# Row products of the scores on 64 rows, four in a burst, and seven PSUM banks in one rotation

## What is computed

```python
def _L0_cond_ref(x, mask, conditioning, Wq, Wk, Wv, Wo, rms_scale, Wc, bc):
    q, k, v = (proj(Wq), proj(Wk), proj(Wv))            # (B, 16, 512, 16)
    scores = jnp.einsum('bhsd,bhtd->bhst', q, k) * scale
    scores = jnp.where(mask[None, None, :, :], -jnp.inf, scores)
    attn = jax.nn.softmax(scores, axis=-1)
    out = jnp.einsum('bhst,bhtd->bhsd', attn, v)
    out = out.transpose(0, 2, 1, 3).reshape(B, S, E)
    out = out @ Wo.T
    ...
```

## Time and profile before

| what | us |
|---|---|
| median of 3 runs | 1162.19 (1161.24 to 1168.41) |
| the profiled execution, its span | 1162.1 |
| attention: first row product to last column product | about 18 to 613 |
| experts and the end | 613 to 1162 |

### The profile page before, as it was taken

How to read it: one execution, slowest core, us unless ns; L and a number is a source line. 1 busy time by engine, 2 the same in 40 slices (tenths; PEclk the granted TensorE clock), 3 DMA queues, 4 the chain that set the end, 5 groups by cost and what they waited for, 6 DMA issues and landing times.

```text
span 1162.1 us, 23399 instructions
## 1 busy us (share of the span) xinstructions
PE 1122.4 (97%) x7520; PEld 763.4 (66%) x7520; DVE 770.8 (66%) x2265; ACT 803.1 (69%) x1752; POOL 512.6 (44%) x837
## 2 busy tenths in 40 slices
PE   8899999999999999998989999999999999999988
PEld 4333434434334343342418999998999999999968
DVE  4877777787887878878745434355555555667747
ACT  2578888787787877877786756655666666666645
POOL 8424135583755837657462365354222223222220
PEclk8999999999999999999999999999999999999999
DMA  8665638367384572843837488856566766723536
GB/s 220 193 195 189 219 100 250 124 215 231 119 257 138 198 235 94 242 157 133 286 101 269 115 309 306 267 120 133 155 193 190 213 193 179 226 48 70 164 91 217
DMA packets 101616, 213.64 MB, mean 184 GB/s; under 512 B 10917, under 2 KB 71341, under 8 KB 93046
## 3 DMA queue, kind: packets, MB, share of 16 engines
q1 hardware_dynamic: 86038, 192.42, 51.1%
q0 software_dynamic: 14304, 18.69, 9.0%
q10 hardware_dynamic: 1152, 1.05, 0.4%
HBM read 239.28 MB, written 74.29 MB: 270 GB/s over the span
## 4 chain that ended last, share of the span: by engine, by line
PE 46%; ACT 3%; issue 1%; DVE 1%; POOL 1%; DMA 1%; another core or an unknown queue 0%; ACTq 0%; POOLq 0%
PE bank L1084 38%; PE bank L1247 1%; PE bank L1189 1%; PE bank L1099 1%; ACT pt L1355 1%; PE bank L1170 1%; DMA x<-yout,rows 1%; PE bank L1113 1%; PE bank L1174 1%; PE bank L1207 1%; PE bank L1282 0%; PE bank L1155 0%; PE bank L1227 0%; ACT full L1433 0%
## 5 line engine op out<-in xcount | busy, mean ns | idle before, releaser
L1628 DVE CUSTOM_DVE_ANT_0 junk<-bank,mneg 128x512 bf16<-128x512 f32 x512 | 333.0, 683 | 119.0 <-PE bank L1155 116.3
L1355 ACT ACTIVATE pt<-bank 128x512 f32<-128x512 f32 x512 | 301.0, 594 | 67.8 <-PE bank L1170 29.7
L1975 POOL DMA_INDIRECT x<-yout,rows x78 | 122.8, 1574 | 292.9 <-ACT yout L1438 249.6
L1084 PE MATMUL bank<-hid,w 128*128 128x256 f32 x1872 | 242.7, 286 | 4.2 <-DVE hid L1776 3.8
L1084 PEld LDWEIGHTS bank<-hid,w 128*128 128x128 f32 x1872 | 229.3, 190 | 6.0 <-issue 4.8
L1776 DVE TENSOR_TENSOR hid<-full,hid 128x256 fp32r<-128x256 f32 x312 | 133.3, 431 | 135.3 <-ACT full L1433 126.8
L1428 ACT ACTIVATE hid<-bank,biases 128x256 fp32r<-128x256 f32 x312 | 149.4, 479 | 91.6 <-PE bank L1084 88.0
L1433 ACT ACTIVATE full<-bank,biases 128x256 f32<-128x256 f32 x312 | 148.7, 477 | 0.0
L1174 PE MATMUL bank<-mneg,identb 128*128 128x512 bf16 x386 | 146.9, 381 | 0.0
L1084 PE MATMUL bank<-rowsT,w 128*128 128x256 f32 x936 | 122.9, 284 | 0.9 <-issue 0.9
L1084 PE MATMUL bank<-w,hid 128*128 128x256 f32 x936 | 121.9, 283 | 1.5 <-DVE hid L1776 1.5
(11 more groups left out here) (184 smaller groups left out, 1445.2 us busy)
## 6 DMA issues: line engine op xcount, KB each, us to landing
w<-split_weights SPq DMA_DIRECT2D x80, 1024.0 KB
w<-split_weights SPq DMA_DIRECT2D x40, 2048.0 KB
split_weights<-w_parts SPq DMA_DIRECT2D x64, 512.0 KB, 3.8
w_parts<-in_W SPq DMA_DIRECT2D x64, 256.0 KB, 4.3
split_parts<-parts SPq DMA_DIRECT2D x28, 384.0 KB, 2.6
rows<-routed SPq DMA_DIRECT2D x39, 258.0 KB, 3.4
stacks<-split_parts SPq DMA_DIRECT2D x36, 256.0 KB, 5.2
qst<-split_parts SPq DMA_DIRECT2D x24, 256.0 KB, 5.3
```

The lines of the kernel that those rows point to most:

```text
L1084: product = T.matmul(ps, w[p], x[q], start=(k == 0 and n == 0), stop=(k == len(weights) - 1 and n == 2))
L1355: A.activation(pt[n % len(pt)][:, :], bank[3 + n % 2][:, :], ACT.Exp, scale=float(D) ** -0.5).then_inc(exped.sem, 1)
L1628: V.tensor_tensor_reduce(junk[n % 2][:, :], bank[n % 3][:, :], mneg[:, 0, st, :], 1.0, FLOOR, ALU.add, ALU.max, rowmax[gi % 2][:, hh, st:s ...
L1975: G.indirect_dma_start(x2_dram, bass.IndirectOffsetOnAxis(ap=rows[j % NS][:, tt, E + 1:E + 2].bitcast(U32), axis=0), yout[j % NY][:, tt], ...
```

## The change

- The row product takes only the first four of the six pairs (`ROW_PAIRS`): 64 rows instead of 96. The heads of a group are laid out in two halves. Heads 0 and 1 have their four pairs on partitions 0 to 63, heads 2 and 3 on 64 to 127. The other two pairs, the shift rows and zeros fill the other half, so that a column product takes 98 rows for heads 0 and 1 as before, and all 128 for heads 2 and 3.
- The four row products of a step `k` are issued one after another, ahead of its column products, in head order 0, 2, 1, 3: alternately on the lower and the upper 64 partitions. For the first two groups they stay single, the lower half's first.
- All products of the attention except "weigh" take banks 0 to 4, 6 and 7 in one rotation (`RING`), in the order in which they are issued. Each waits for its bank's last user seven places back. A seed is chosen so that the last user was a column product, and ScalarE writes it up to three column products ahead.
- With the layout, the DMAs into `qst` and `kst` are split in two halves (24 instead of 12 per sequence, 2 instead of 1 for each group's maxima), and POOL writes six more constants. For the first two groups the projections of the second sequence come one `k` earlier, and splitting and turning of maxima move by a few places.

```diff
+ROW_PAIRS = 4
+KR = ROW_PAIRS * D
+ROW_HEADS = (0, 2, 1, 3)
+RING = (0, 1, 2, 3, 4, 6, 7)
+SEED_AHEAD = 3
-SEEDED_HEADS = (3,), (0,), (3,), (0,)
-FIRST_PROJECTS = range(3, 7)
+FIRST_PROJECTS = range(2, 6)
...
+def slot_of(h):
+    g, hh = divmod(h, GH)
+    return hh // 2 * (H // 2) + g * (GH // 2) + hh % 2
+
+def pair_rows(half, r):
+    if r < ROW_PAIRS:
+        first, step = half * KR + r, ROW_PAIRS
+    else:
+        first, step = (KR, KR // 2)[half] + r - ROW_PAIRS, len(PAIRS) - ROW_PAIRS
+    return slice(first, first + (D - 1) * step + 1, step)
+
+def shift_rows_of(half):
+    return slice(0, SHIFTS) if half else slice(KQ, KQ + SHIFTS)
...
+    first_rows = [(i, hh, st) for n in range(2) for i in range(2) for st in range(ST) for hh in (2 * n, 2 * n + 1)]
...
+            if 2 <= i < GROUPS:
+                out.append(("rows", i, k))
             for n in range(GH):
-                if i < GROUPS:
-                    out.append(("row", i, n, k))
-                if k == 0 and n == 0 and 0 <= i - 1 < GROUPS:
+                if i < 2:
+                    found = first_rows[(i * ST + k) * GH + n]
+                    out.extend((("one_row", *found), ("row", *found)))
+                elif i < GROUPS:
+                    out.append(("row", i, ROW_HEADS[n], k))
+                if n == 0 and ((i, k) == (1, 2) or k == 0 and 2 <= i <= GROUPS):
                     out.append(("split_maxima", i - 1))
...
-            if k == 1 and 0 <= i - 1 < GROUPS:
-                out.append(("maxima_rows", i - 1))
+                if (i, k, n) == (1, 2, 2) or (k, n) == (1, 3) and 2 <= i <= GROUPS:
+                    out.append(("maxima_rows", i - 1))
...
+    def ring_before(step):
+        n = ring_place[step] - len(RING)
+        return ring_users[n] if n >= 0 else None
+
+    seed_after = {}
+    for gi in range(1, GROUPS):
+        for kt in range(ST):
+            choices = []
+            for hh in range(GH):
+                before_it = ring_before(("col", gi, kt, hh))
+                if before_it[0] == "col":
+                    choices.append((col_place[gi, kt, hh] - col_place[before_it[1:]], -hh))
+            if choices:
+                ahead, hh = max(choices)
+                place = col_place[gi, kt, -hh]
+                seed_after[cols_at[place - min(ahead, SEED_AHEAD)]] = gi, kt, -hh
...
+    def ring_bank(step):
+        user = ring_before(step)
+        return bank[RING[ring_place[step] % len(RING)]], user and evicted(user)
...
                     for r in range(n, len(PAIRS), STACK_STEPS):
-                        start((qst, kst)[qk][b % 2][r:KQ:len(PAIRS), :, :].rearrange("d (a h) s -> d a (h s)", a=2),
-                              split_dram[b, qk, PAIRS[r][qk]].rearrange("(a d h) s -> d a (h s)", a=2, d=D)).then_inc(dma_stack[qk], 16)
+                        for half in range(2):
+                            start((qst, kst)[qk][b % 2][pair_rows(half, r), half * (H // 2):(half + 1) * (H // 2), :],
+                                  split_dram[b, qk, PAIRS[r][qk]][half * P:(half + 1) * P, :].rearrange("(d h) s -> d h s", d=D)
+                                  ).then_inc(dma_stack[qk], 16)
...
+        def row_product(gi, hh, st):
+            b, half, at_slot = gi // NG, hh // 2, slot_of(gi % NG * GH + hh)
+            ps = take(ring_bank(("row", gi, hh, st)))
+            stacks_loaded(pe, b, half)
+            rows = slice(half * KR, (half + 1) * KR)
+            T.matmul(ps[:, :], qst[b % 2][rows, at_slot, st * P:(st + 1) * P],
+                     kst[b % 2][rows, at_slot, :], start=True, stop=True).then_inc(row_scored.sem, 1)
...
-                n = row_place[gi, hh, st]
-                if n >= 3:
-                    pe.wait_ge(*max_found.at(rows_at[n - 3]))
-                stacks_loaded(pe, b, h // (H // 2))
-                T.matmul(bank[n % 3][:, :], qst[b % 2][0:KQ, h, st * P:(st + 1) * P], kst[b % 2][0:KQ, h, :],
-                         start=True, stop=True).then_inc(row_scored.sem, 1)
+            elif name == "one_row":
+                row_product(*at)
+            elif name == "rows":
+                gi, st = at
+                for hh in ROW_HEADS:
+                    row_product(gi, hh, st)
             elif name == "col":
                 gi, kt, hh = at
-                ps = bank[3 + n % 2]
+                stack = slice(0, P) if hh // 2 else slice(0, KQ + SHIFTS)
+                ps, freed = ring_bank(step)
                 seed = (gi, kt, hh) in seeded.value
                 if seed:
                     pe.wait_ge(*seeded.at((gi, kt, hh)))
                 else:
-                    pe.wait_ge(*(exped.at(cols_at[n - 2]) if n >= 2 else v_ready.at((0, ST - 1))))
+                    pe.wait_ge(*freed)
```

More of the change, by code:

```diff
@@ L1 @@
+import struct
 import numpy as np
@@ L816, in stacks_loaded @@
             for qk in range(2):
-                queue.wait_ge(dma_stack[qk], 16 * len(PAIRS) * b)
+                queue.wait_ge(dma_stack[qk], 2 * 16 * len(PAIRS) * b)
     def first_rows(qk, half, part, r):
         assert PAIRS[r][qk] == part
-        return ((qst, kst)[qk][0][r:KQ:len(PAIRS), half * (H // 2):(half + 1) * (H // 2), :], parts[qk][:, half, part, :])
+        return ((qst, kst)[qk][0][pair_rows(half, r), half * (H // 2):(half + 1) * (H // 2), :], parts[qk][:, half, part, :])
     def last_col(b):
@@ L966, in sync_program @@
                     sp.wait_ge(*last_col(b - 2))
-                start(qst[b % 2][KQ:KQ + SHIFTS, gi % NG * GH:(gi % NG + 1) * GH, :], mrow[gi % 2][:, :]).then_inc(dma_mrow[gi % 2], 16)
+                sp.wait_ge(constants_made, CONSTANTS)
+                for half in range(2):
+                    first, n = slot_of(gi % NG * GH + half * GH // 2), SHIFTS * GH // 2
+                    start(qst[b % 2][shift_rows_of(half), first:first + GH // 2, :],
+                          mrow[gi % 2][half * n:(half + 1) * n, :]).then_inc(dma_mrow[gi % 2], 16)
             elif name == "pads":
@@ L1817, in constant, with shift_constants @@
             made[0] += 1
+        def shift_constants(i):
+            halves = [slice(half * (H // 2), (half + 1) * (H // 2)) for half in range(2)]
+            for stacks in (kst, qst):
+                constant(G.memset, stacks[i][0:KR // 2, halves[1], :].bitcast(F32), 0.0)
+            for half in range(2):
+                constant(G.memset, kst[i][shift_rows_of(half), halves[half], :].bitcast(F32), TWO_MINUS_ONES)
         G.memset(ident[:, :], 0.0).then_inc(ident_made, 1)
```

84 lines of the change are left out of this document (46 added, 38 removed).

## The result

The changed kernel takes 1192.51 us (median of 4 runs, 1192.12 to 1195.23), the kernel before 1162.82 on the same chip: ratio 1.0251, 95% interval 1.0225 to 1.0276. It is **slower by 2.5%**. The forecast was 1138. The profiled execution has a span of 1190.4 us, 28.3 more than before.

A forecast was written before the change was run, and what follows sets the result against it. The prediction took TensorE to bound the attention, streaming 96% of its middle part. From 1162.1 us it took 18 (bursts), 0 (rotation), 4 (end) and 2 (start), giving 1138 us, range 1125 to 1150.

The forecast's parts named there:

- The bound: Middle of the attention: TensorE streams 96% of the time, idles about 20 of 480 us, and the readers wait.
- The burst, 0.73 us (0.65 to 0.85): Four paired 64-row products on TensorE, with mode entry and exit, take 0.73 us instead of 0.876.
- Rivals 3: Each mode change on TensorE drains the product's tail: 0.86 us per burst, total 1154 us; chance 0.10.
- 4 (no pairs, 1.09): 64-row products do not run side by side: 1.09 us per burst, total 1181 us; chance 0.09.
- The gain, 18 us: Attention: 0.15 us saved in each of 120 bursts shortens the whole by 18 us (bounds 3 and 27).
- One rotation, 0 us (+10 to -15): Seven banks shared in the attention: new waits of 9 us and 11 us of removed thin waits cancel.
- The wait that I priced: Third column product behind a projection waits 0.33 us for its bank; 28 projections make 9 us.
- Rival 2: The rotation's waits in the attention give back the burst's gain, 24 us; total 1155 to 1164 us; chance 0.14.
- my own sign: TensorE idle growing to 1.5 us per group, with `rests`, `max_rows` or `o_ready` before a column product, shows rival 2.
- The start, -2: Start of the attention, where DVE sets the pace: more maxima queued ahead save 2 us (0 to 3).
- the end, -4: Last two groups of the attention: TensorE runs ahead on seven banks, ACT's gaps close, saving 4 us (2 to 5).
- The signs that I had named: Row products start in pairs, 17.5 us per group in the middle, TensorE idle near 0.8 us per group.

The follow-up runs named there:

- e5: The rotation-only kernel (e1) with the four row products in one burst from the third group on, still on 96 rows: 1200.1 us, 1.0279.
- e6: The changed kernel with each burst of four row products cut into two bursts of two: 1184.67 us, 1.0166.
- e7: The changed kernel with a step's side product (projection and the like) moved between the first and second pair of column products: 1179.73 us, 1.0097.
- e9: The changed kernel with two bursts of two and the side product behind the first column product: 1181.34 us, 1.0139.
- e1: The kernel before with only the one rotation of seven banks, rows and columns alternating on 96 rows: 1171.33 us, 1.0054.
- e8: The changed kernel with VectorE's rest of a projection ahead of the step's first row maximum instead of behind it: 1202.74 us, 1.0317.
- e11: e7 with two steps of the gate's chain put later in VectorE's order for five of eight sequences: 1182.16 us, 1.0149.
- e10: The kernel before with the side product moved between column products, as in e7, as a control: ratio 1.0085.
- e4: The changed kernel with the heads of a burst in the order 0, 1, 2, 3: ratio 1.0285.

## Why the prediction was wrong

**The bound.** Right for the kernel before: TensorE sets its pace. What I did not read from the earlier trace rows is how close behind the others came. VectorE and ScalarE were at 78 and 80% and were fed rows and columns in turn. I took their 99.8 and 40 us of waiting as slack. It was slack in sum, but not in any one place. (TensorE's own thin waits, which I put at 20 us in the middle part, were 9.)

**The burst, 0.73 us (0.65 to 0.85).** TensorE pays 0.63, just under the lower bound: entry 0.09, exit about 0.10 (0.54 less two steps of 0.22). Rivals 3 (the tail drained, 0.86) and 4 (no pairs, 1.09) are out. "TensorEngine Tiling (Array Packing)" in the Trainium skill, Key Properties, says that a change of mode drains the engine. The traces price the two ways together at 0.19 us.

**The gain, 18 us. This is the step that failed.** I multiplied 0.15 us by 120 bursts, as if work taken from the bound came off the end. The sentence behind it, that the work on VectorE and ScalarE "keeps its order and size", so that they "do not become the bound", counted busy time alone. What the edit moved was the rows' place among the columns. Before, row and column stood in turn, and a column with its mask came about every 0.66 us, near ScalarE's 0.6. Now four maxima fall due at once, while the columns come bunched behind the burst at 0.44; a side product (up to 1.8) and the next burst (0.63) then stand together without one, and in every second step a weighing (1.84) stands ahead of them, with a single column product between. TensorE's queue, strictly in order, waits for readers that are late. e5 shows that the burst's order makes the loss alone (78.3 against 74.1 us per sequence), and e6 that cutting the burst in two gives 18 of 29 us back. That the readers run dry in the gap between columns and are late after it is my reading: e7 fits it in sign, e9 speaks against the gap as the cause.

**One rotation, 0 us (+10 to -15).** Right for alternating products: e1's attention ends when it did before, and TensorE's idle time falls from 9 to 6 us. The wait that I priced, a column product on a projection's bank, exists under bursts: 0.42 us in the row above and 0.54 in the mean (11.4 / 21), where I had 0.33. But it is a symptom. e8 took most of it away and gained nothing.

**Rival 2.** It named the right signals (`rests`, `max_rows`, routing, in front of column products) and the wrong cause, and by my own sign (idle over 1.5 us per group with these signals) it would have been called right. It stopped at 1164 because I let its waits at most cancel the gain. Nothing bounds them so: the changed kernel waits more than its burst saves. My one slower case was a failure of the pairs. No case of mine had a faster TensorE and a slower kernel.

**The start, -2, and the end, -4.** The start gives nothing: the first weighing stands at 52.18 us against 52.22, with a granted clock of 0.84 in 18:43.4 where it was 0.87. The end is wrong in sign. From the last common count to the last mask product the stretch took 36.6 us (35.2 before). There VectorE works through the last tables, one row maximum between two of their steps, and TensorE waits for those maxima (after, three of four such places):

```profile
611.36 0.39 PE L1244 MATMUL bank<-qst,kst 128*128 128x512 bf16 x1 [1.15 <-DVE rowmax L1703]
613.57 0.39 PE L1244 MATMUL bank<-qst,kst 98*128 98x512 bf16 x1 [1.60 <-DVE rowmax L1703]
...
616.75 0.61 PE L1244 MATMUL bank<-qst,kst 128*128 128x512 bf16 x1 [1.16 <-DVE rowmax L1703]
```

A column product that waits for a row maximum could not exist before: rows and columns had banks of their own. Here the waits that the shared banks allow are 4.7 us in four places, once. Behind them the granted clock fell: TensorE was busy 2.28 of the 7 us from 610, and then

```profile
617.00:623.00 6.00, 6.00 (x23) 1.18 (x22) 3.66 (x15) 1.69 (x4) 4.03 (x8) 0.53 0.19 66
```

the clock is near its lower level (1.2 GHz), and two weighings cost 3.55 us (617.72 to 621.27) instead of 1.84. So 1.7 us at least of this stretch's time are the clock, more than the 1.4 by which it is longer. In 20:100 the clock is 0.94 where it was 0.96. In the middle, where the 4.2 us per sequence are lost, it is 1.00 in both, and the clock does not explain those.

**What would show it.** The signs that I had named did their work: bursts in pairs, yes; 17.5 us per group, no (78.0 / 4 = 19.5 on average over a sequence); idle near 0.8 us per group, no (about 1.9).

**What stays open.** That the order of issue makes the loss is shown (e5); what in the order does it is not. Which waits close at 78.0 us was not isolated. Two single suspects were taken away without gain (e8, e11), and the two spreading moves do not add (e9). The gap without columns is at most a part of it, by e9. Four maxima due at once, or the burst's need of four free banks (rival B of e11), remain; e6 eases both. Why e7's move costs the kernel before 11 us of attention (e10) is open too.

## What to carry to other kernels

Before you shorten work on the busiest engine, look at what its order feeds. If two others stand at 80% behind it, the order of their inputs is part of the speed, and an edit that gathers work into bursts for the sake of one engine has to be priced on the readers: how many items fall due at once, how many banks must be free for that, and the longest stretch without an item. Price a bound by the interval of a landmark that comes once per period, and read each stage's end beside the whole time: here the part behind the attention moved by up to 16 us between kernels that do not touch it. An interval that repeats to a hundredth does not tell what sets it: it did so in the changed kernel (78.0) and also in e10 (75.34), where TensorE idled 13 us of 480.

The Trainium skill says it in "TensorEngine Tiling (Array Packing)", PSUM Bottleneck: tiling speeds up TensorE but not the evacuation of PSUM. This case agrees only in part: tiling cut four products from 0.876 to 0.63 us and the readers did not follow, far below the four times that its sentence speaks of. But the same bursts on 96 rows, with no tiling at all (e5), lose as much, so here it is the order, not TensorE's speed, that hurts.

## What the runs showed of the hardware

- Two products of 64 rows on the two halves of the array, 512 columns each, run side by side: four take 0.54 us to the next product (some 40 of the bursts between 240 and 560 us; a burst on 96 rows takes 0.86), two take 0.32.
- The order within the burst does not matter: heads on the same half next to each other (e4) give the same 0.54, where I had expected about 0.22 more. Two products for one half and then two for the other overlap as well as alternating ones.
- A pair alone is worth almost nothing. 0.09 + 0.32 = 0.41 us stand against 0.44 for two plain products, and 0.63 against 0.876 for four. Between two and four nothing was measured.
